# A gated cross-attention and mixture-of-experts block: preparation of the later batches spread anew over the engines, and batch 1 attended tile by tile

## The chip, the cores and the metric

One core of a Trainium2 chip runs the whole program. The metric is the device time of one execution in microseconds (us), lower is better. Engines are named as in the profile: PE is TensorE, DVE is VectorE, ACT is ScalarE, POOL is GpSimd, SP is SyncE, which here only starts transfers.

## The reference

x is 4 batches of 256 tokens with 256 features; ctx has the same shape.

```python
h  = layernorm(x)
xq = dequant(fp8(h))    # one scale for 128 features of a token
wq = dequant(fp8(ctx))  # one scale for a block of 128 x 128
x  = x + tanh(g_xattn) * einsum('emk,enk->emn', xq, wq)

h     = layernorm(x)
probs = softmax(h @ gate_w.T)       # 8 experts, top 4, renormalised
y_e   = (silu(h @ wg_e.T) * (h @ wu_e.T)) @ wd_e.T   # inner width 176
sh    = (silu(h @ swg.T) * (h @ swu.T)) @ swd.T      # inner width 704
out   = sum_e comb_e * y_e + sigmoid(h @ shared_gate_w.T) * sh
x     = x + tanh(g_ffn) * out
```

## The kernel before

The order on every engine is written out by hand, and semaphores join the engines. The work has two layers.

**Preparation**, once for each batch b of 0 to 3, two tiles of 128 tokens each. For x: moments (`stats_x`, DVE), inverse roots (`roots`, POOL), centring (`centre`, ACT), the largest magnitudes (`max_x`, DVE), scales (`scales_x`, DVE), scaling to the range of the 8-bit format (`scale_x`, ACT, four instructions). Then rounding to the grid of that format in float32: the exponent is masked out (`exponents_x`, DVE, L624), turned into a "magic number", 1.5 * 2^20 times the power of two, and this number is added and subtracted. For batches 1 to 3 of x and 0, 2, 3 of ctx the magic number is one more DVE instruction (`magic_x` L679, `magic_ctx` L642) and the addition and subtraction are two (`round_x` L685, L686, `round_ctx` L648, L649). For batch 0 of x and batch 1 of ctx ACT makes the magic number (`magic`, L377), and two DVE instructions of the scalar_tensor_tensor kind round with it (`rounded`, L628, L629). ctx has `max_ctx`, then a maximum over partitions by way of PE for two batches at once (`ctx_block_max`, `ctx_spread_max` on PE, `block_max_ctx`, `scales_ctx` on DVE), `scale_ctx` on ACT, and the same rounding.

The rounded x is transposed on PE (`transpose_xq`, L992), copied (`copy_xqt`, ACT, L381) and multiplied with ctx (`attend`, L1005) into two PSUM banks, one for each half k of the features. ACT scales the product of k = 0 into y2 (`residual0`, L388), DVE scales that of k = 1 and adds x (`residual1`, L710), DVE adds both (`residual_sum`, L717), and the second layernorm follows (`stats_x1`, `inverse_std1` on POOL L287, `norm_x1` L729), with transposes of x1 and of its normalised form y2 on PE. For batches 0 and 1 all this is a chain ahead of everything else, the prologue. In it `keep_clock_up(count)` (L1102) issues matrix products whose result nobody uses.

**Units.** The 2112 inner columns of all experts and of the shared layer are cut into 17 chunks, `UNITS`; they run twice, each time for half of the tokens (512, batches 0 and 1, then 2 and 3). Unit n has, on PE,

```python
            def unit(n):
                gate(n)
                up(n)
                down(n - 1)
```

each of six matrix products of 512 columns in float32 (three passes of high and low parts over two blocks, L1039, L1145 to L1153). Chunk 5 of each half, `SHORT`, has six and four in all. ACT makes the high parts of the weights (`high_gu` L434, `high_d` L438; `front` and `middle` issue them) and of the activations (`high_a`, L455), and the silu (L450); POOL makes the low parts of the weights (`low_gu` L293, `low_d` L299); DVE weighs the silu with the router's share (`mixed`, L788), multiplies by the up product (`gated`, L801; both are issued by `acts`) and makes the low part of the result (`low_a`, L810; for the short chunk the two are L797 and L807). What binds PE to them: `gate(n)` waits for `gu_lo_done` of its own weights and, as there is one bank GATE, for `mixed(n - 1)`; `down(n)` waits for `a_hi_done` and later `a_lo_done`.

The preparation of batches 2 and 3 is interleaved with units 2 to 15 in program order on each engine. The shared layer's result is weighed and added to x1t in `weigh_shared` (L829) and `add_shared` (L834), at units 6, 10 and 16 for the first half and at unit 23 for the second.

## Time and profile before

| | |
|---|---|
| median of 3 runs | 185.47 us (185.4 to 186.02) |
| the profiled execution | 185.45 us |
| its span in the profile | 183.0 us |
| PE busy | 158.4 us (87%) |
| DVE busy | 130.6 us (71%) |
| ACT busy | 101.9 us (56%) |
| POOL busy | 78.3 us (43%) |

The span is from the first to the last instruction that the profile shows; 2.45 us of the execution lie outside it. Times in the rows are from the start of the span. A matrix product's duration holds its way through the array, so that rows of PE overlap: what one costs is the distance between two starts. A row of the timeline is: start, duration, engine, line, operation, written tile and read tiles, count, and in brackets the idle time of the engine before it with what ended it.

### The profile page before, as it was taken

The page shows a single profiled execution, that of the slowest core. Times are in us where ns is not written, and L with a number is a line of the kernel's source. Part 1 is how long each engine was busy: PE and PEld are TensorE (multiplying, and loading weights), DVE is VectorE, ACT ScalarE, POOL GpSimd, SP SyncE. Part 2 cuts the span into 40 slices and gives each one's busy share as a digit, 9 for nine tenths or more (in the row PEclk, how much of TensorE's full clock was granted, in tenths as well). Part 3 has the DMA queues.
Part 4 walks back from the last instruction along what each step waited for, and adds up shares of the span by engine and source line. Part 5 has one row for each costly group of instructions (what it writes and reads, how often), then busy time and mean ns, then how long its engine had stood idle before and what let it go on. Part 6 is the DMA issues. An engine that isn't in the chain of part 4 may idle for free.

```text
span 183.0 us, 2355 instructions
## 1 busy us (share of the span) xinstructions
PE 158.4 (87%) x711; PEld 123.1 (67%) x711; DVE 130.6 (71%) x281; ACT 101.9 (56%) x220; POOL 78.3 (43%) x91
## 2 busy tenths in 40 slices
PE   0023999999996989998999999999998999999992
PEld 0011356877874867776788888888886888888871
DVE  1899994686878999999988755863478645554553
ACT  2568724488666865455765544595553555445430
POOL 4211244155764444440765443544554654544410
PEclk9999999999999999999999999999999999999999
DMA  4599900000299993222222222601999200000003
GB/s 130 147 407 400 378 4 0 5 0 4 97 264 231 343 402 131 86 59 86 86 90 86 86 88 86 206 0 53 217 266 324 89 5 0 0 0 0 0 0 115
DMA packets 11488, 22.74 MB, mean 124 GB/s; under 512 B 1986, under 2 KB 3010, under 8 KB 11476
## 3 DMA queue, kind: packets, MB, share of 16 engines
q1 hardware_dynamic: 10900, 22.07, 37.8%
q10 hardware_dynamic: 576, 0.52, 1.0%
q8 instruction: 5, 0.08, 0.2%
q14 instruction: 7, 0.06, 0.1%
HBM read 21.51 MB, written 1.09 MB: 123 GB/s over the span
## 4 chain that ended last, share of the span: by engine, by line
PE 53%; DVE 31%; issue 6%; ACT 5%; DMA 2%; POOL 1%; DVEq 1%; POOLq 0%
PE bank L1039 34%; DVE bank L801 4%; PE bank L1145 3%; DVE a_lo L810 3%; DVE silu L788 3%; PE bank L1149 2%; PE bank L1147 2%; PE bank L1146 2%; PE bank L1153 2%; PE bank L1152 2%; ACT a_hi L455 2%; DVE bn L596 2%; DMA x<-xs 2%; DVE x1t L834 2%; DVE x L710 1%
## 5 line engine op out<-in xcount | busy, mean ns | idle before, releaser
L293 POOL TENSOR_TENSOR w_lo<-w_raw,w_hi 128x512 fp32r<-128x512 f32 (+1 forms) x34 | 42.8, 1258 | 65.2 <-ACT w_hi L434 61.1
L1039 PE MATMUL bank<-h_hi,w_hi 128*128 128x512 f32 x130 | 52.2, 402 | 3.5 <-DVE silu L788 3.4
L1039 PE MATMUL bank<-h_hi,w_lo 128*128 128x512 f32 x130 | 50.8, 391 | 0.0
L1039 PE MATMUL bank<-h_lo,w_hi 128*128 128x512 f32 x130 | 50.7, 390 | 0.0
L455 ACT ACTIVATE a_hi<-bank 128x512 fp32r<-128x512 f32 (+1 forms) x34 | 20.3, 597 | 41.3 <-DVE bank L801 40.7
L299 POOL TENSOR_TENSOR w_lo<-w_raw,w_hi 128x256 fp32r<-128x256 f32 x34 | 26.1, 769 | 16.3 <-ACT w_hi L438 16.3
L1039 PEld LDWEIGHTS bank<-h_hi,w_hi 128*128 128x128 f32 x130 | 24.4, 188 | 10.7 <-issue 5.4
L801 DVE TENSOR_TENSOR bank<-silu,bank 128x512 f32<-128x512 f32 x32 | 22.2, 694 | 12.8 <-PE bank L1039 9.6
L810 DVE TENSOR_TENSOR a_lo<-bank,a_hi 128x512 fp32r<-128x512 f32 x32 | 22.0, 689 | 11.7 <-ACT a_hi L455 11.5
L1039 PEld LDWEIGHTS bank<-h_hi,w_lo 128*128 128x128 f32 x130 | 24.4, 188 | 5.3
L1039 PEld LDWEIGHTS bank<-h_lo,w_hi 128*128 128x128 f32 x130 | 24.5, 188 | 4.5
L788 DVE TENSOR_TENSOR silu<-bank,mix_b 128x512 f32<-128x512 f32 x22 | 15.1, 686 | 11.5 <-ACT bank L450 11.5
L434 ACT ACTIVATE w_hi<-w_raw 128x512 fp32r<-128x512 f32 (+1 forms) x34 | 20.8, 612 | 0.0
L450 ACT ACTIVATE bank<-bank 128x512 f32<-128x512 f32 x22 | 12.9, 585 | 10.0 <-PE bank L1039 10.0
L438 ACT ACTIVATE w_hi<-w_raw 128x256 fp32r<-128x256 f32 x34 | 13.9, 409 | 0.0
L1145 PE MATMUL bank<-a_hi,w_hi 128*128 128x512 f32 x32 | 12.6, 395 | 0.2 <-ACT a_hi L455 0.2
L1147 PE MATMUL bank<-a_hi,w_hi 128*128 128x512 f32 x32 | 12.5, 390 | 0.0
L1149 PE MATMUL bank<-a_lo,w_hi 128*128 128x512 f32 x32 | 12.5, 390 | 0.0
L1153 PE MATMUL bank<-a_lo,w_hi 128*128 128x512 f32 x32 | 12.5, 390 | 0.0
L1152 PE MATMUL bank<-a_hi,w_lo 128*128 128x512 f32 x32 | 12.5, 389 | 0.0
L1146 PE MATMUL bank<-a_hi,w_lo 128*128 128x512 f32 x32 | 12.5, 389 | 0.0
L976 PE MATMUL bank<-eye,amax_c 128*8 128x128 f32 x2 | 0.6, 324 | 9.4 <-DVE amax_c L590 9.4
(137 smaller groups left out, 215.3 us busy)
## 6 DMA issues: line engine op xcount, KB each, us to landing
w_raw<-w_full SPq DMA_DIRECT2D x32, 384.0 KB, 7.6
mix_b<-rows_dram SPq DMA_DIRECT2D x8, 256.0 KB, 6.5
out_t<-fin SPq DMA_DIRECT2D x4, 256.0 KB, 2.1
mix_b<-rows_dram SPq DMA_DIRECT2D x4, 224.0 KB, 6.1
mix_b<-rows_dram SPq DMA_DIRECT2D x4, 192.0 KB, 5.9
mix_b<-rows_dram SPq DMA_DIRECT2D x4, 160.0 KB, 5.9
x<-xs SPq DMA_DIRECT2D x2, 256.0 KB, 6.6
cw<-ctx_t SPq DMA_DIRECT2D x2, 256.0 KB, 7.0
```

Of the source, the lines that this page charges most:

```text
L293: nc.gpsimd.tensor_tensor(w_lo[:, n % 2, 0:cols], w_raw[:, n % RING, 0:cols], w_hi[:, n % 2, 0:cols].bitcast(F32), ALU.subtract).then_inc( ...
L299: nc.gpsimd.tensor_tensor(w_lo[:, n % 2, GU:WC], w_raw[:, n % RING, at:at + D], w_hi[:, n % 2, GU:WC].bitcast(F32), ALU.subtract).then_inc ...
L434: nc.scalar.activation(w_hi[:, n % 2, 0:cols], w_raw[:, n % RING, 0:cols], ACT.Copy).then_inc(gu_hi_done, 1)
L455: nc.scalar.activation(a_hi[0:rows, n % 2, :], UP[n % 2][0:rows, :], ACT.Copy).then_inc(a_hi_done, 1)
L788: nc.vector.tensor_tensor(silu[:, n % 2, :], GATE[:], mix_b[:, c, :], ALU.mult).then_inc(mixed_done, 1)
L801: nc.vector.tensor_tensor(UP[n % 2][:], silu[:, n % 2, :], UP[n % 2][:], ALU.mult).then_inc(act_done, 1)
L810: nc.vector.tensor_tensor(a_lo[:, n % 2, :], UP[n % 2][:], a_hi[:, n % 2, :].bitcast(F32), ALU.subtract).then_inc(a_lo_done, 1)
L1039: last = nc.tensor.matmul(out, w[k][a], x_of[k][b], start=(start and k == 0 and i == 0), stop=(stop and k == blocks - 1 and i == 2))
L1145: nc.tensor.matmul(OUT[0][:], w_hi[:, n % 2, cols[0]], a_hi[:, n % 2, :], start=start, stop=False)
L1146: nc.tensor.matmul(OUT[0][:], w_lo[:, n % 2, cols[0]], a_hi[:, n % 2, :], start=False, stop=False)
L1147: nc.tensor.matmul(OUT[1][:], w_hi[:, n % 2, cols[1]], a_hi[:, n % 2, :], start=start, stop=False)
L1149: done = nc.tensor.matmul(OUT[0][:], w_hi[:, n % 2, cols[0]], a_lo[:, n % 2, :], start=False, stop=stop)
```

## The change

- **Rounding.** `exponents_x` and, for batches 1 to 3, `exponents_ctx` now hand over to ACT, which makes the magic number (`magic_x`, `magic_ctx`), and `round_by_magic_x` and `round_by_magic_ctx` on DVE round with two scalar_tensor_tensor instructions. Five DVE instructions (x of batches 1, 2, 3, ctx of 2, 3) go and five on ACT come. ctx of batch 0 stays as it was.
- **Batch 1.** `attend_by_tiles(1)` multiplies token tile by token tile, into four bank halves in four banks (P1, P2, P0, OUT[1]), and reports each tile. Transposes of x1 of batches 0 and 1 go to UP[1] and UP[0]. `keep_clock_up` ahead of it has two products in place of four.
- **Sum of batch 0.** POOL does it (`residual_sum_0`) in place of DVE.
- **Weights.** `high_gu(0)`, `high_d(0)` and `high_gu(1)` stand later on ACT, behind `residual0(0)` and `residual0(1)`.
- **Batches 2 and 3.** The steps of preparation are placed anew in units 1 to 12 on DVE, ACT, POOL and PE. `add_shared` stands behind `low_a(16)` for the first half, and for the second its two instructions stand in units 24 and 25 in place of both ahead of unit 24.

```diff
-        ATT = ((UP[0], UP[1]), (P1, P2), (P0, P2), (P0, P2))
-        X1T = (OUT[1], P0, P1, P0)
+        ATT = ((UP[0], UP[1]), None, (P0, P2), (P0, P2))
+        ATT1 = ((P1, P2), (P0, OUT[1]))
+        X1T = (UP[1], UP[0], P1, P0)
         Y2T = (OUT[0], None, P1, P2)
         Y2T1 = (P1, OUT[1])
         LOGIT = (P0, P1)
...
         mixed_done, act_done = sem("mixed_done"), sem("act_done")
         a_hi_done, a_lo_done = sem("a_hi_done"), sem("a_lo_done")
         out_done, out_read, fin_done = sem("out_done"), sem("out_read"), sem("fin_done")
+
+        def attended(b):
+
+            return (1, 3, 4, 5)[b]
+
+        def att_view(b, k, jj):
...
+            def residual_sum_0():
+                pool.wait_ge(part0_done, 1)
+                pool.wait_ge(res0_ready, 1)
+                nc.gpsimd.tensor_tensor(x1[:, tile_slice(0), :], x1[:, tile_slice(0), :], y2[:, tile_slice(0), :], ALU.add)\
+                    .then_inc(x1_ready[0], 1)
+
             def low_gu(n):
...
             low_gate_w()
-            pool.wait_ge(cq_ready[1], 1)
+            residual_sum_0()
             low_gu(0)
             inverse_std1(0)
...
             low_d(3)
-            weights(4)
+            low_gu(5)
             roots(3)
+            low_d(4)
             for n in range(5, 13):
                 weights(n)
...
-            def magic(power, needs):
-
-                a.wait_ge(needs, 1)
+            def magic(power, powers, count):
+
+                a.wait_ge(powers, count)
                 a.wait_ge(least_filled, 1)
                 nc.scalar.activation(power, power, ACT.Relu, bias=least[:], scale=MAGIC).then_inc(magic_done, 1)
+
+            def magic_x(b, count):
+                magic(xe[:, tile_slice(b)].rearrange("p j k c -> p (j k c)"), power_x, count)
+
+            def magic_ctx(b, count):
+                magic(ce[:, b].rearrange("p k n c -> p (k n c)"), power_c, count)
 
             def copy_xqt(b):
                 a.wait_ge(xqt_psum, b + 1)
                 nc.scalar.activation(xqt[:, b], qt_view(b), ACT.Copy).then_inc(xqt_ready, 1)
 
             def residual0(b):
-                a.wait_ge(att_ready, b + 1)
                 a.wait_ge(deq_ready, b // HB + 1)
                 for jj, j in enumerate(tiles(b)):
+                    a.wait_ge(att_ready, attended(b) - (1 if b == 1 and jj == 0 else 0))
                     for n in range(2):
-                        last = nc.scalar.activation(y2[:, j, n * P:(n + 1) * P], ATT[b][0][:, jj * D + n * P:jj * D + (n + 1) * P],
-                                                    ACT.Copy, scale=deq[:, j, 0, n:n + 1])
+                        ns = slice(n * P, (n + 1) * P)
+                        last = nc.scalar.activation(y2[:, j, ns], att_view(b, 0, jj)[:, ns], ACT.Copy, scale=deq[:, j, 0, n:n + 1])
                 last.then_inc(res0_ready, 1)
 
             def copy_x1t(b):
...
-            magic(xe[:, tile_slice(0)].rearrange("p j k c -> p (j k c)"), power_x)
+            magic_x(0, 1)
             scale_ctx(0)
             scale_x(1)
             scale_ctx(1)
+            magic_x(1, 2)
             copy_xqt(0)
             high_gate_w()
+            magic_ctx(1, 1)
+            copy_xqt(1)
+            residual0(0)
             high_gu(0)
+            residual0(1)
             high_d(0)
             high_gu(1)
-            magic(ce[:, 1].rearrange("p k n c -> p (k n c)"), power_c)
-            copy_xqt(1)
-            residual0(0)
-            residual0(1)
             copy_x1t(0)
             copy_x1t(1)
...
             high_a(5)
+            scale_ctx(2)
             front(6)
             middle(6)
-            scale_x(3)
+            scale_x(2)
             high_a(6)
             front(7)
             middle(7)
-            scale_ctx(2)
+            magic_ctx(2, 2)
             high_a(7)
+            scale_x(3)
             front(8)
             middle(8)
+            magic_x(2, 3)
+            high_a(8)
             scale_ctx(3)
-            high_a(8)
             front(9)
             middle(9)
-            copy_xqt(2)
+            magic_x(3, 4)
             high_a(9)
             front(10)
             middle(10)
+            magic_ctx(3, 3)
+            copy_xqt(2)
             high_a(10)
             front(11)
-            copy_xqt(3)
             middle(11)
             high_a(11)
             residual0(2)
-            unit(12)
+            front(12)
+            middle(12)
+            copy_xqt(3)
+            high_a(12)
             front(13)
             middle(13)
...
-            def rounded(out, val, power, done):
-
+            def rounded(out, val, power, magics, done):
+
+                v.wait_ge(magic_done, magics)
                 after(did(nc.vector.scalar_tensor_tensor(val, power, LEAST, val, ALU.add, ALU.add)))
                 nc.vector.scalar_tensor_tensor(out, val, LEAST, power, ALU.subtract, ALU.subtract).then_inc(done, 1)
+
+            def round_by_magic_x(b, magics):
+                flat = "p j k c -> p (j k c)"
+                rounded(xq[:, tile_slice(b)].rearrange(flat), xc[:, tile_slice(b)].rearrange(flat),
+                        xe[:, tile_slice(b)].rearrange(flat), magics, xq_ready)
+
+            def round_by_magic_ctx(b, magics):
+                flat = "p k n c -> p (k n c)"
+                rounded(cq[:, b].rearrange("p k c -> p (k c)"), cw[:, b].rearrange(flat), ce[:, b].rearrange(flat),
+                        magics, cq_ready[b])
 
             def exponents_ctx(b):
                 v.wait_ge(ctx_scaled, b + 1)
                 last = exponents(ce[:, b].rearrange("p k n c -> p (k n c)"), cw[:, b].rearrange("p k n c -> p (k n c)"))
...
-
-            def round_x(b, magic_step):
-                flat = "p j k c -> p (j k c)"
-                val, mag = xc[:, tile_slice(b)].rearrange(flat), xe[:, tile_slice(b)].rearrange(flat)
...
-                after(did(nc.vector.tensor_tensor(val, val, mag, ALU.add)))
-                nc.vector.tensor_tensor(xq[:, tile_slice(b)].rearrange(flat), val, mag, ALU.subtract).then_inc(xq_ready, 1)
+                last.then_inc(power_x, 1)
 
...
+                    v.wait_ge(att_ready, attended(b) - (1 if b == 1 and jj == 0 else 0))
                     for n in range(2):
                         ns = slice(n * P, (n + 1) * P)
-                        last = nc.vector.scalar_tensor_tensor(x1[:, j, ns], ATT[b][1][:, jj * D + n * P:jj * D + (n + 1) * P],
+                        last = nc.vector.scalar_tensor_tensor(x1[:, j, ns], att_view(b, 1, jj)[:, ns],
                                                               deq[:, j, 1, n:n + 1], x[:, j, ns], ALU.mult, ALU.add)
+                if b == 0:
+                    last.then_inc(part0_done, 1)
+                    return None
                 return did(last)
 
...
-                    .then_inc(x1_ready, 1)
+                    .then_inc(x1_ready[b], 1)
 
             def stats_x1(b):
-                v.wait_ge(x1_ready, b + 1)
+                v.wait_ge(x1_ready[b], 1)
                 moments(1, x1, b)
                 nc.vector.tensor_scalar(ve1[:, tile_slice(b)], mv[:, 1, tile_slice(b), 1], LN_EPS, None, ALU.add)\
...
-            v.wait_ge(magic_done, 1)
-            flat_x, flat_c = "p j k c -> p (j k c)", "p k n c -> p (k n c)"
-            rounded(xq[:, tile_slice(0)].rearrange(flat_x), xc[:, tile_slice(0)].rearrange(flat_x),
-                    xe[:, tile_slice(0)].rearrange(flat_x), xq_ready)
+            round_by_magic_x(0, 1)
             mag_c0 = magic_ctx(0, exponents_ctx(0))
+            exponents_x(1)
             round_ctx(0, mag_c0)
-            mag_x1 = magic_x(1, exponents_x(1))
-            round_x(1, mag_x1)
             exponents_ctx(1)
             dequant_scales(0)
-            v.wait_ge(magic_done, 2)
-            rounded(cq[:, 1].rearrange("p k c -> p (k c)"), cw[:, 1].rearrange(flat_c), ce[:, 1].rearrange(flat_c), cq_ready[1])
-            residual_sum(0, residual1(0))
+            round_by_magic_x(1, 2)
+            round_by_magic_ctx(1, 3)
+            residual1(0)
             part_1 = residual1(1)
...
+            max_ctx(2)
+            max_ctx(3)
             acts(2)
             low_a(2)
             stats_x(2)
-            max_ctx(2)
             acts(3)
             low_a(3)
+            block_max_ctx(1)
             stats_x(3)
             acts(4)
+            scales_ctx(1)
             low_a(4)
-            max_ctx(3)
             scales_x(2, max_x(2))
             acts(5)
-            max_x_3 = max_x(3)
             low_a(5)
-            block_max_ctx(1)
-            scales_x(3, max_x_3)
+            scales_x(3, max_x(3))
             acts(6)
             weigh_shared(0)
             low_a(6)
-            scales_ctx(1)
+            exponents_ctx(2)
             acts(7)
-            exp_x2 = exponents_x(2)
-            mag_x2 = magic_x(2, exp_x2)
+            exponents_x(2)
+            dequant_scales(1)
             low_a(7)
-            exp_x3 = exponents_x(3)
-            mag_x3 = magic_x(3, exp_x3)
             acts(8)
-            round_x(2, mag_x2)
+            round_by_magic_ctx(2, 4)
             low_a(8)
-            exp_c2 = exponents_ctx(2)
-            mag_c2 = magic_ctx(2, exp_c2)
+            exponents_x(3)
             acts(9)
-            round_x(3, mag_x3)
+            round_by_magic_x(2, 5)
             low_a(9)
-            exp_c3 = exponents_ctx(3)
-            mag_c3 = magic_ctx(3, exp_c3)
+            exponents_ctx(3)
             acts(10)
-            round_ctx(2, mag_c2)
+            round_by_magic_x(3, 6)
             low_a(10)
-            dequant_scales(1)
-            shared_0 = [add_shared(0, 0)]
             acts(11)
-            round_ctx(3, mag_c3)
+            round_by_magic_ctx(3, 7)
             low_a(11)
             part_2 = residual1(2)
...
             gated(16)
-            shared_0.append(add_shared(0, 1))
             low_a(16)
+            shared_0 = [add_shared(0, 0), add_shared(0, 1)]
             acts(17)
             low_a(17)
...
             low_a(UNITS + SHORT + 1)
-            shared_1 = [add_shared(1, 0), add_shared(1, 1)]
-            for n in range(UNITS + SHORT + 2, 2 * UNITS):
+            acts(UNITS + SHORT + 2)
+            shared_1 = [add_shared(1, 0)]
+            low_a(UNITS + SHORT + 2)
+            acts(UNITS + SHORT + 3)
+            shared_1.append(add_shared(1, 1))
+            low_a(UNITS + SHORT + 3)
+            for n in range(UNITS + SHORT + 4, 2 * UNITS):
                 unit(n)
             finish(1, shared_1)
...
+            def attend_by_tiles(b):
+
+                pe.wait_ge(xqt_ready, b + 1)
+                pe.wait_ge(cq_ready[b], 1)
+                for jj in range(BT):
+                    for k in range(KC):
+                        last = nc.tensor.matmul(att_view(b, k, jj), xqt[:, b, k, jj * P:(jj + 1) * P],
+                                                cq[:, b, k, :], start=True, stop=True)
+                    last.then_inc(att_ready, 1)
 
             def transpose_tokens(b, src, dst, done):
...
                 pe.wait_ge(y2_ready, b + 1)
...
             transpose_xq(1)
-            keep_clock_up(4)
-            attend(1)
+            keep_clock_up(2)
+            attend_by_tiles(1)
             keep_clock_up(9)
             transpose_x1(0)
...
             transpose_comb(0)
+            ctx_block_max(1)
             unit(3)
-            unit(4)
-            unit(5)
-            ctx_block_max(1)
-            unit(6)
+            gate(4)
+            up(4)
             ctx_spread_max(1)
-            unit(7)
-            unit(8)
-            gate(9)
+            down(3)
+            for n in range(5, 10):
+                unit(n)
+            gate(10)
             transpose_xq(2)
-            up(9)
-            down(8)
-            unit(10)
-            transpose_xq(3)
+            up(10)
+            down(9)
             gate(11)
             up(11)
             attend(2)
             down(10)
-            unit(12)
+            gate(12)
+            transpose_xq(3)
+            up(12)
+            down(11)
             gate(13)
             transpose_x1(2)
```

## Rows read from the trace of the kernel before

**Rows 1.** The page: engines (part 1) and two groups of instructions (part 5).

```profile
PE 158.4 (87%) x711; PEld 123.1 (67%) x711; DVE 130.6 (71%) x281; ACT 101.9 (56%) x220; POOL 78.3 (43%) x91
...
L455 ACT ACTIVATE a_hi<-bank 128x512 fp32r<-128x512 f32 (+1 forms) x34 | 20.3, 597 | 41.3 <-DVE bank L801 40.7
```

**Rows 2.** Who PE waited for: us in total, times, longest.

```profile
PE bank L1039 <- DVE silu L788: 3.4, 5, 1.1
```

**Rows 3.** Chain that ended last, in order of time: start, us, what.

```profile
112.61 2.72 PE bank L1039 x12
```

**Rows 4.** Timeline of PE, the stretches in which it stood still.

```profile
56.92 0.47 PE L1140 MATMUL bank<-a_hi,w_hi 128*128 128x512 f32 x1 [0.52 <-DVE a_hi L807]
...
59.59 0.47 PE L1039 MATMUL bank<-h_hi,w_hi 128*128 128x512 f32 x1 [1.12 <-DVE silu L788]
...
70.51 0.40 PE L992 MATMUL bank<-eye_b,xq 128*128 128x128 bf16 x4 [0.36 <-DVE xq L686]
```

**Rows 5.** Timeline of DVE, units 8 and 9.

```profile
67.72 0.68 DVE L788 TENSOR_TENSOR silu<-bank,mix_b 128x512 f32<-128x512 f32 x1
...
69.04 0.68 DVE L685 TENSOR_TENSOR xc<-xc,xe 128x512 f32<-128x512 f32 x1
...
70.97 0.96 DVE L624 TENSOR_SCALAR ce<-cw 128x512 int32<-128x512 int32 x1
71.96 0.84 DVE L642 TENSOR_SCALAR ce<-ce 128x512 f32<-128x512 f32 x1
72.73 0.68 DVE L788 TENSOR_TENSOR silu<-bank,mix_b 128x512 f32<-128x512 f32 x1
```

**Rows 6.** Timeline of POOL, the same stretch.

```profile
70.36 1.29 POOL L293 TENSOR_TENSOR w_lo<-w_raw,w_hi 128x512 fp32r<-128x512 f32 x1 [2.84 <-ACT w_hi L434]
71.61 0.92 POOL L299 TENSOR_TENSOR w_lo<-w_raw,w_hi 128x256 fp32r<-128x256 f32 x1
```

**Rows 7.** Timeline of DVE and ACT, unit 5.

```profile
53.45 0.60 DVE L662 SCALAR_TENSOR_TENSOR safe_x<-amax_x,root 128x4 f32<-128x4 f32 x1
...
54.30 1.28 ACT L370 ACTIVATE xc<-xc,mul_x 128x128 f32<-128x128 f32 x4 [1.19 <-DVE mul_x L665]
```

**Rows 8.** Timeline of all engines, the prologue.

```profile
9.75 0.72 ACT L377 ACTIVATE xe<-xe,least 128x512 f32<-128x512 f32 x1
...
13.17 1.26 ACT L370 ACTIVATE xc<-xc,mul_x 128x128 f32<-128x128 f32 x4
13.76 0.43 DVE L642 TENSOR_SCALAR ce<-ce 128x512 f32<-128x512 f32 x1
...
19.01 0.69 DVE L628 SCALAR_TENSOR_TENSOR cw<-ce,cw 128x512 f32<-128x512 f32 x1 [0.24 <-ACT ce L377]
...
20.35 1.12 DVE L710 SCALAR_TENSOR_TENSOR x<-bank,deq,x 128x128 f32<-128x128 f32 x4
20.51 1.26 POOL L293 TENSOR_TENSOR w_lo<-w_raw,w_hi 128x512 fp32r<-128x512 f32 x1 [3.26 <-DVE cq L629]
21.50 0.82 DVE L717 TENSOR_TENSOR x<-x,y 128x512 f32<-128x512 f32 x1
...
23.28 0.73 DVE L596 BATCH_NORM_STATS2 bn<-x 128x6 f32<-128x256 f32 x2
...
27.28 0.73 DVE L729 TENSOR_SCALAR y<-x,mv,rstd 128x256 f32<-128x256 f32 x2 [0.27 <-POOL rstd L287]
```

**Rows 9.** Timeline of PE, the prologue.

```profile
18.35 1.91 PE L1102 MATMUL bank<-xqt,eye_b 128*128 128x512 bf16 x4
...
24.76 1.03 PE L1102 MATMUL bank<-xqt,eye_b 128*128 128x512 bf16 x4
...
29.08 0.47 PE L1075 MATMUL bank<-h_hi,gate_hl 128*128 128x512 f32 x1
```

**Rows 10.** Timeline of DVE and of PE, unit 23 and the start of gate(24).

```profile
137.35 2.50 DVE L834 SCALAR_TENSOR_TENSOR x1t<-fin,g_tanh,x1t 128x512 f32<-128x512 f32 x2
...
140.60 0.47 PE L1039 MATMUL bank<-h_hi,w_hi 128*128 128x512 f32 x1 [0.78 <-DVE silu L788]
```

More of the change, by code:

```diff
@@ L166, in flamingo_gated_block @@
         att_ready, res0_ready = sem("att_ready"), sem("res0_ready")
-        x1_ready, y2_ready = sem("x1_ready"), sem("y2_ready")
+        x1_ready, y2_ready = [sem(f"x1_ready{b}") for b in range(B)], sem("y2_ready")
+        part0_done = sem("part0_done")
         var1_ready, rstd1_ready = sem("var1_ready"), sem("rstd1_ready")
@@ L178, in flamingo_gated_block @@
         out_done, out_read, fin_done = sem("out_done"), sem("out_read"), sem("fin_done")
+        def attended(b):
+            return (1, 3, 4, 5)[b]
+        def att_view(b, k, jj):
+            return ATT1[jj][k][:, 0:D] if b == 1 else ATT[b][k][:, jj * D:(jj + 1) * D]
         def tiles(b):
@@ L512, in _ @@
             middle(5)
-            scale_x(2)
             high_a(5)
+            scale_ctx(2)
             front(6)
             middle(6)
-            scale_x(3)
+            scale_x(2)
             high_a(6)
@@ L633, in exponents_ctx @@
                 last = exponents(ce[:, b].rearrange("p k n c -> p (k n c)"), cw[:, b].rearrange("p k n c -> p (k n c)"))
-                if b == 1:
+                if b > 0:
                     last.then_inc(power_c, 1)
@@ L1001, in attend @@
                 if b == 3:
-                    pe.wait_ge(x1_ready, 3)
+                    pe.wait_ge(x1_ready[2], 1)
                 for k in range(KC):
                     for jj in range(BT):
-                        last = nc.tensor.matmul(ATT[b][k][:, jj * D:(jj + 1) * D], xqt[:, b, k, jj * P:(jj + 1) * P],
+                        last = nc.tensor.matmul(att_view(b, k, jj), xqt[:, b, k, jj * P:(jj + 1) * P],
                                                 cq[:, b, k, :], start=True, stop=True)
                 last.then_inc(att_ready, 1)
+            def attend_by_tiles(b):
[3 more added lines that the diff above has]
+                    for k in range(KC):
+                        last = nc.tensor.matmul(att_view(b, k, jj), xqt[:, b, k, jj * P:(jj + 1) * P],
+                                                cq[:, b, k, :], start=True, stop=True)
+                    last.then_inc(att_ready, 1)
             def transpose_tokens(b, src, dst, done):
@@ L1015, in transpose_x1 @@
             def transpose_x1(b):
-                pe.wait_ge(x1_ready, b + 1)
+                pe.wait_ge(x1_ready[b], 1)
                 if b == 2:
@@ L1028, in transpose_y2_by_blocks @@
                 pe.wait_ge(y2_ready, b + 1)
-                pe.wait_ge(x1t_copied, 1)
                 for k in range(KC):
```

10 lines of the change are left out of this document (removed).

## The prediction

> **What bounds the kernel now.** I read the page first, then who PE waited for, then PE's timeline for the places, then DVE, ACT and POOL around each place. PE is busy 158.4 of 183.0 us, the next engine DVE 130.6 [rows 1]. Twelve products in a row take 2.72 us, 0.227 us each [rows 3], so a full unit of 18 costs PE 4.08 us. PE is therefore the bound wherever its rows follow one another at this distance. It stands still in three stretches.
>
> First, the prologue: the first product that does lasting work in the units starts at 29.08 [rows 9]. The chain there is DVE's, from rounding through attention, the sum, the second layernorm.
>
> Second, units 5 to 12. PE waits 3.4 us in five places for `mixed` [rows 2], 0.78 of it in unit 24 [rows 10], which leaves 2.6 us in four places here, the longest 1.12. To these come 0.52 ahead of `down(5)` and 0.36 ahead of `transpose_xq(2)` [rows 4]. A product's row is 0.39 long where it costs 0.227, so each place loses 0.16 more than its idle time: 2.6 + 0.52 + 0.36 + 6 x 0.16 = 4.5 us. The reader is to see why in DVE's rows: from `mixed` of unit 8 to that of unit 9 are 72.73 - 67.72 = 5.01 us [rows 5], with no gap, against PE's 4.08. DVE is the bound of these units.
>
> Third, unit 24: 0.78 + 0.16 = 0.94 us lost, behind two `add_shared` that took 2.50 us [rows 10].
>
> **A price that matters throughout: DVE and POOL exclude each other.** The exponent step at 70.97 takes 0.96 us and ends at 71.93; POOL's `low_gu` has run since 70.36 and ends at 71.65 [rows 5, 6]. The same kind of instruction takes 0.43 with POOL idle [rows 8]. So it started only when POOL was through. In the other direction `low_d` takes 0.92 beside the DVE step at 71.96. A small step of `scales_x` is held 0.60 us in unit 5 [rows 7]. But `residual1`, whose product is read from PSUM, takes 1.12 with POOL's 20.51 to 21.77 on top of it [rows 8]. The Trainium skill, SBUF — State Buffer, section Who interferes with whom, has the rule: a DVE instruction in a two-port mode or with two SBUF inputs and a GpSimd instruction that reads SBUF lock each other out for a whole instruction; with at most one SBUF input and outside those modes it doesn't. By that rule the trace agrees. The rule speaks against expecting anything from scalar_tensor_tensor for its own sake: both roundings read two SBUF tensors and stay exposed.
>
> **Part A, the prologue.** After x of batch 0 is rounded, DVE masks ctx 0 and makes its magic number from 13.76 to 14.20 [rows 8], as before. The mask of x 1 now comes next and needs `scale_x(1)`, which ends at 13.17 + 1.26 = 14.43 [rows 8]: it starts at 14.46. It lies under the wait between steps, and `round_ctx(0)` follows with 0.35 + 0.72 + 0.60: the mask of ctx 1 starts at 16.13. Then 0.35, then `dequant_scales` to about 17.05. The magic numbers of x 1 and ctx 1 cost ACT 0.72 each [rows 8]; ACT makes the first from 15.5 and the second from 17.0, both before DVE asks. So DVE runs four rounding instructions without a gap, a pair in 20.35 - 19.01 = 1.34 us [rows 8]: 17.05 + 2.68 = 19.7. Before, `residual1(0)` started at 20.35; it gains 0.65: the removed magic instruction (0.46 with its hand-over), the 0.24 wait for ACT at 19.01, and small change. POOL's low part of the gate weights may hold one of them 0.2 to 0.3.
>
> `residual1(1)` can follow at 20.8: the products of batch 1 need xq 1 (18.45), its transposes, 0.6 of copying on ACT and then cq 1 at 19.8, and its first tile is there at about 20.4. What moved later on ACT is hidden: the copy of batch 0 comes 0.6 later and attention 0 with it, at 16.8, but its readers start at 19.6; `high_gu(0)` ends by 21.3, and the low part that PE wants at 28 lies on POOL in between.
>
> The sum of batch 0 takes DVE 0.82 [rows 8]; POOL has no such instruction in the trace. Nearest: POOL's subtraction of the same size, 1.26 with POOL alone. Below, 0.82 if POOL were as quick as DVE; above, 2.0 if a DVE instruction holds it first. I take 1.28, since kind and size are equal: 20.85 to 22.15. DVE's own sum stood at 21.50, but its statistics began only at 23.28, since `residual1(1)` was in between [rows 8]. They now begin at 22.15, 1.1 earlier. Then `low_gu(0)` runs on POOL to 23.4 and can hold the small step and `residual_sum(1)` for some 0.2. So the normalisation of batch 1, at 27.28 [rows 8], comes 0.9 to 1.1 earlier.
>
> PE must keep up. Four keep-up products before attention 1 took 1.91 us, 0.43 apart, and four later 1.03, 0.22 apart, both read as start to last end [rows 9]: the first run at the 1.2 GHz level, the later at 2.4, though the granted clock is shown full throughout. With two in place of four, attention 1 goes at 19.8 instead of 20.57. If the following nine stay slow to their end they take 3.9 and PE reaches the transposes of y2 about 0.3 late. I take 0.95 for part A; 0.3 (both POOL's sum and PE late) and 1.3 (no collision) are its bounds.
>
> **Part B, units 2 to 12.** Removed from DVE are four magic instructions here. In the unit of rows 5 it is 72.73 - 71.96 = 0.77 of the 5.01. The rest is 4.24 with the blocked mask, or 3.7 with an unblocked one, against PE's 4.08 and 0.2 to 0.4 of transposes or attention that the units carry. DVE stops being the bound, on the mean. The pass of maxima of ctx moves to unit 1 and 2, where DVE has waits; its small PE instructions cost as much in the new place. In unit 5, `gated(5)` no longer has `scale_x(2)` (1.28, [rows 7]) between it and `high_a(5)`, and DVE's second maximum is gone from ahead of `low_a(5)`: the 0.52 + 0.16 before `down(5)` goes.
>
> What is late next. (1) `mixed(6)` waits for its silu on ACT, which now stands behind `high_a(5)`, the 1.28 us of `scale_ctx(2)` and a weight instruction: following ACT from `gated(5)` on I get `gate(7)` about 0.4 late, against 1.12 + 0.16. (2) `transpose_xq(2)` stands behind `gate(10)`, which starts when `mixed(9)` ends and takes six products, 1.36 us. DVE in that time does `gated(9)` and the rounding pair, 0.65 + 1.34 = 2.0: PE waits 0.6, and more if POOL holds the pair. (3) Units 8 to 10: the weights of the next unit come behind a scaling or a magic number on ACT, and then need 1.29 on POOL; I allow 0.5 in all. So 1.5 of the 4.5 stays: gain 3.0. Bounds: 4.5 when nothing stays, 1.0 when each of the four magic numbers keeps ACT waiting for the mask and each rounding meets POOL once.
>
> ACT has 2.4 us of its own work for a unit at most (four instructions of at most 0.6, [rows 1]), plus 1.28 for a scaling, plus 0.72 for a magic number: 4.4 as an upper bound, with the narrow instructions less. That is close to a unit, and the reason why I keep 1.5.
>
> **Part C, unit 24.** One `add_shared` for a unit, each behind `gated` and ahead of a `low_a` whose result `down` wants more than a microsecond later. Two blocked ones took 2.50; one of 0.7 to 1.3 fits into the 1.2 that DVE waits in such a unit and that low part's slack. Gain 0.9, bounds 0 and 0.94. The first half's pair behind `low_a(16)` is hidden: DVE waits for PE there.
>
> **Sum.** 0.95 + 3.0 + 0.9 = 4.85 us. The profiled execution took 185.45, the median is 185.47; 185.45 - 4.85 = 180.6.
>
> **Rivals.**
> - *Locks and hand-overs eat half of part B.* For: DVE steps grew from 0.43 to 0.96 [rows 5] and the mask must now pass through ACT, where DVE once went on by itself. Against: DVE has other work between mask and rounding now. B falls to 1.0 to 1.7, A to 0.6: 181.9 to 184.
> - *Nothing is late.* If DVE runs ahead of `gate(10)` by 0.6 and ACT's order is as loose as its 56%: B is 4.2 to 4.5, total 178.7 to 179.6.
> - *Slower: ACT becomes the bound of units 6 to 11.* The place is a magic number ahead of `high_a(n)`: ACT waits for the mask, the mask waits for POOL, and `high_a`, the next weights and the next silu are queued behind it, on which POOL and DVE wait in turn. With A and C gained (1.85), the six units must lose 2.4 us more than now to end slower by 0.56, 0.4 in each on top of the 5.01 of unit 8, so that with the magic instruction gone from DVE each such wait must exceed about 1.2 us beyond its slack. The longest hold in these rows is 0.53 (0.96 against 0.43). Time then: 186 to 187.
> - *The change does not do what it says*: the prologue's gain is taken back by a slower sum on POOL, and in units 5 to 12 one wait replaces another. 185.
>
> **How the numbers follow.** Forecast 0.55 (its own range 179.6 to 181.9), nothing late 0.12, half of B 0.20, no change 0.05, slower 0.08. 178.8 to 183.6 leaves out the last two and an edge of two others. A measurement here can tell about 0.3%, 0.56 us: faster 0.87, same 0.05, slower 0.08.
>
> **What would show it.** Right: the first product of the units at about 28.1; `gate(13)` 3 to 4.5 us earlier than before; `mixed` to `mixed` below 4.5 us in units 8 to 10; no idle ahead of `gate(24)`; the rest shifted. Wrong: PE waits of 1 us and more for `a_hi` or `w_lo` in units 7 to 10, ACT idle ahead of L377, POOL's sum over 1.5 us, or keep-up products 0.43 apart up to the first real one.

## The result and the profile after

The changed kernel took 179.1 us (median of 4 runs, 178.6 to 179.66) against 185.44 us before: ratio 0.9656, 95% interval 0.9617 to 0.9695. It is 6.3 us faster (5.7 to 7.1). The forecast was 180.6, within 178.8 to 183.6, faster by 4.85. On another chip the same kernel later gave 0.9663 (0.9633 to 0.9693).

The page of the changed kernel, parts 1 and 5, and who PE waited for:

```profile
span 177.2 us, 2353 instructions
...
PE 155.8 (88%) x708; PEld 122.9 (69%) x709; DVE 123.4 (70%) x275; ACT 105.2 (59%) x225; POOL 79.0 (45%) x92
...
L477 ACT ACTIVATE a_hi<-bank 128x512 fp32r<-128x512 f32 (+1 forms) x34 | 20.3, 597 | 32.0 <-DVE bank L829 30.9
```

```profile
PE bank L1015 <- DVE xq L659: 3.4, 3, 2.4
...
PE bank L1071 <- POOL w_lo L308: 0.2, 1, 0.2
```

The wait of the products for `mixed`, 3.4 us in five places [rows 2], is gone; PE's 3.4 us for rounded x are 2.4 in the prologue, 0.7 there again and 0.3 in unit 10. DVE is 7.2 us less busy, ACT 3.3 more, POOL 0.7 more [rows 1].

The profiled execution took 178.96 us, 6.49 less than the 185.45 before; its span is 5.8 less, 177.2 against 183.0. The other 0.7 us lies outside the span, where the four executions of the changed kernel have anything from 1.8 to 2.5 us, so it is no gain that the trace can place. The span divides at three products. All times below are read the way the prediction did: a product costs the distance between two starts.

PE's timeline of the changed kernel: the first product of the units, `gate(3)`, the two small products of `ctx_spread_max(1)`, then the two places where it still stands still, then `gate(13)`:

```profile
28.41 0.47 PE L1107 MATMUL bank<-h_hi,gate_hl 128*128 128x512 f32 x1
...
41.70 0.47 PE L1071 MATMUL bank<-h_hi,w_hi 128*128 128x512 f32 x1
...
48.59 0.28 PE L1003 MATMUL bank<-eye,blk_w 128*128 128x8 f32 x2
48.73 0.48 PE L1177 MATMUL bank<-a_hi,w_hi 128*128 128x512 f32 x1
...
56.32 0.39 PE L1173 MATMUL bank<-a_hi,w_lo 128*128 128x512 f32 x1
...
56.91 0.50 PE L1071 MATMUL bank<-h_hi,w_hi 128*128 128x512 f32 x1 [0.20 <-POOL w_lo L308]
57.25 0.39 PE L1071 MATMUL bank<-h_lo,w_hi 128*128 128x512 f32 x1
...
70.85 0.39 PE L1071 MATMUL bank<-h_hi,w_lo 128*128 128x512 f32 x1
...
71.53 0.40 PE L1015 MATMUL bank<-eye_b,xq 128*128 128x128 bf16 x4 [0.29 <-DVE xq L659]
...
83.56 0.39 PE L1071 MATMUL bank<-h_hi,w_hi 128*128 128x512 f32 x1
```

And the same points of the kernel before, where rows 4 do not show them:

```profile
42.37 0.47 PE L1039 MATMUL bank<-h_hi,w_hi 128*128 128x512 f32 x1
...
57.69 0.40 PE L1141 MATMUL bank<-a_hi,w_lo 128*128 128x512 f32 x1
58.07 0.39 PE L980 MATMUL bank<-eye,blk_w 128*128 128x8 f32 x2
...
88.22 0.47 PE L1039 MATMUL bank<-h_hi,w_hi 128*128 128x512 f32 x1
```

- *Prologue.* The first product comes at 28.41 in place of 29.08 [rows 9]. But the first rounding started later, since the first x landed later: 12.31 in place of 11.93. From that rounding to the first product it is 16.10 us in place of 17.15: 1.05 gained.
- *Units 3 to 12.* From `gate(3)` (42.37) to `gate(13)` (88.22) it was 45.85 us; now it is 83.56 - 41.70 = 41.86: 4.0 gained. What is left of the stalls is 56.91 - 56.32 - 0.227 = 0.36 ahead of `gate(7)`, 71.53 - 70.85 - 0.227 = 0.45 ahead of `transpose_xq(2)`, and 0.05 and 0.04 ahead of `gate(9)` and `gate(10)`: 0.9 in all. Read in the same way, the kernel before loses 4.8, not the 4.5 of the prediction. The difference is at `gate(7)`: from 57.69 to 59.59 [rows 4] there lies one product (0.227) and the two small ones, which cost 48.73 - 48.59 = 0.14 where nothing stalls, so 1.53 us are lost there, where 1.12 + 0.16 were counted.
- *Unit 24.* The 0.94 us stall [rows 10] is gone.

Together 6.0 of the trace, or 5.6 of the 5.8 by which the span is shorter, since the first rounding came 0.38 later.

DVE's timeline of the changed kernel, `mixed` of units 7 to 9 and the steps of unit 8 between them:

```profile
60.15 0.68 DVE L816 TENSOR_TENSOR silu<-bank,mix_b 128x512 f32<-128x512 f32 x1
...
64.39 0.69 DVE L816 TENSOR_TENSOR silu<-bank,mix_b 128x512 f32<-128x512 f32 x1 [1.36 <-ACT bank L472]
...
65.72 0.77 DVE L658 SCALAR_TENSOR_TENSOR cw<-ce,cw 128x512 f32<-128x512 f32 x1
...
67.74 0.42 DVE L653 TENSOR_SCALAR xe<-xc 128x512 int32<-128x512 int32 x1
...
68.65 0.69 DVE L816 TENSOR_TENSOR silu<-bank,mix_b 128x512 f32<-128x512 f32 x1 [0.48 <-ACT bank L472]
```

From `mixed` to `mixed` it is now 4.2 to 4.3 us, where it was 5.01 [rows 5], and DVE waits for ACT's silu 1.36 and 0.48 us: it is no longer the bound.

### The profile page after: what moved, and what is told of

Same layout as the page of the kernel before. It is cut to its first block, busy times and chain, and to the rows that moved or that the text cites. A ratio compares the mean times of both kernels' runs of the same rounds, so it can differ in the third digit from the quotient of the medians.

```text
span 177.2 us, 2353 instructions
## 1 busy us (share of the span) xinstructions
PE 155.8 (88%) x708; PEld 122.9 (69%) x709; DVE 123.4 (70%) x275; ACT 105.2 (59%) x225; POOL 79.0 (45%) x92
## 4 chain that ended last, share of the span: by engine, by line
PE 60%; DVE 20%; ACT 9%; issue 5%; DMA 2%; POOL 2%; DVEq 1%; POOLq 0%
PE bank L1071 36%; DVE bank L829 3%; PE bank L1177 3%; PE bank L1181 3%; PE bank L1179 3%; PE bank L1178 3%; PE bank L1184 3%; PE bank L1185 3%; DMA x<-xs 2%; DVE bn L625 2%; ACT cw L378 2%; DVE a_lo L838 2%; DVE silu L816 2%; ACT a_hi L477 1%; ACT xc L386 1%
## 5 line engine op out<-in xcount | busy, mean ns | idle before, releaser
L314 POOL TENSOR_TENSOR w_lo<-w_raw,w_hi 128x256 fp32r<-128x256 f32 x34 | 25.5, 750 | 17.0 <-ACT w_hi L460 17.0
L625 DVE BATCH_NORM_STATS2 bn<-x 128x6 f32<-128x256 f32 x16 | 5.9, 412 | 4.8 <-DMA x<-xs 4.4
```

Of the source, the lines that this page charges most:

```text
L314: nc.gpsimd.tensor_tensor(w_lo[:, n % 2, GU:WC], w_raw[:, n % RING, at:at + D], w_hi[:, n % 2, GU:WC].bitcast(F32), ALU.subtract).then_inc ...
```

## The experiments

All ratios are to the kernel before, measured on the same chip; the changed kernel stood at 0.9656 and 0.9663, 0.001 is about 0.19 us.

### The three parts, each alone

**Prologue alone.** The changed kernel with units 1 to 16 and the shared layer as before.

```diff
 # units: the lists of all engines as before, magic_x and magic_ctx of batches 2 and 3 on VectorE
-            exponents_x(2)
+            exp_x2 = exponents_x(2)
+            mag_x2 = magic_x(2, exp_x2)
...
-            round_by_magic_x(2, 5)
+            round_x(2, mag_x2)
```

> Only the prologue of the changed kernel (rounding of x 1 by ScalarE's magic number, batch 1 by tiles, the sum of batch 0 on GpSimd, later weights); units and shared layer as before. Additive theory: the new kernel's first product came 1.05 us earlier counted from the first rounding, so 1.0 to 1.1 us faster than before, 184.4. Rival, that the units' start is set by something else and gives it back: 185.2 or more.

Measured: 184.25 us against 185.29, ratio 0.9954 (0.9930 to 0.9978), median difference 1.0 us.

**Unit 24 alone.** The kernel before with

```diff
-            shared_1 = [add_shared(1, 0), add_shared(1, 1)]
-            for n in range(UNITS + SHORT + 2, 2 * UNITS):
+            acts(UNITS + SHORT + 2)
+            shared_1 = [add_shared(1, 0)]
+            low_a(UNITS + SHORT + 2)
+            acts(UNITS + SHORT + 3)
+            shared_1.append(add_shared(1, 1))
+            low_a(UNITS + SHORT + 3)
+            for n in range(UNITS + SHORT + 4, 2 * UNITS):
                 unit(n)
```

> Only the two add_shared of the second half in units 24 and 25. Additive theory: the 0.94 us stall ahead of gate(24) goes and nothing else moves, 184.5. Rival, that each add_shared is blocked by POOL and stalls its own unit: 185.0 to 185.5.

Measured: 184.29 us, 0.9947 (0.9922 to 0.9971), 1.0 us faster. DVE's timeline of this kernel:

```profile
139.70 0.75 DVE L834 SCALAR_TENSOR_TENSOR x1t<-fin,g_tanh,x1t 128x512 f32<-128x512 f32 x1
...
143.78 0.75 DVE L834 SCALAR_TENSOR_TENSOR x1t<-fin,g_tanh,x1t 128x512 f32<-128x512 f32 x1
```

Two instructions take 1.5 us in place of 2.50 [rows 10]. Behind `gated` they do not meet POOL; together, ahead of the unit, both did (POOL's low parts ran from 136.87 to 139.30, the pair from 137.35 to 139.85). PE has no idle time ahead of `gate(24)` in this kernel, nor in the changed one.

**Units alone.** The kernel before with the units' lists of all engines and the four magic numbers on ACT as in the changed one, prologue and unit 24 as before.

```diff
 # units 1 to 16: the lists of all engines as in the changed kernel
-            mag_x2 = magic_x(2, exp_x2)
...
+            round_by_magic_ctx(2, 3)
```

> Only units 2 to 16 as in the changed kernel (the four magic numbers on ScalarE and all placements there); prologue and unit 24 as before. Additive theory: what A (1.05) and C (0.94) leave of the 6.3 us, so 4.2 to 4.4 us faster, 181.1. Rival, that part B was worth the predicted 3.0 and A or C more: 182.4.

Measured: 180.75 us, 0.9757 (0.9725 to 0.9790), 4.5 us faster. So the parts are worth 1.0, 1.0 and 4.5, 6.5 in sum against 6.3 for the whole: they add up, within what can be measured (each of the first two is known to some 0.4 us, the third to 0.6). The additive theory stands, and part B is where the forecast was too low. In the trace of this kernel `gate(3)` to `gate(13)` takes 84.33 - 42.49 = 41.84 us, as in the changed kernel, 4.0 less than before.

### Inside the units: less work on DVE, or another place for it?

**Placement without the magic numbers.** The changed kernel with

```diff
-            exponents_ctx(2)
+            mag_c2 = magic_ctx(2, exponents_ctx(2))
...
-            round_by_magic_ctx(2, 4)
+            round_ctx(2, mag_c2)
 # and likewise x of batches 2 and 3 and ctx of batch 3; ScalarE's four magic numbers go
```

> The changed kernel with the four magic numbers of batches 2 and 3 back on VectorE right behind their masks (and rounding in two tensor_tensor), at the new places. If taking work off VectorE is what freed the units: each of units 6 to 10 has 0.5 to 0.9 us more on VectorE, over TensorE's 4.08, and 1.5 to 2.5 us come back: 180.6 to 181.6. Rival, that the new placement alone does it: within 0.5 us of the changed kernel, 179.1 to 179.6.

Measured: 179.93 us, 0.9713 (0.9681 to 0.9746), some 1.0 us slower than the changed kernel (0.9713 against 0.966, the mean of its two ratios). The intervals overlap, but the spans of all four executions are 178.0 to 178.2, those of the changed kernel 176.7 to 177.2, and in the trace `gate(3)` to `gate(13)` takes 84.64 - 41.58 = 43.06 us, 1.2 more than there. That lies between the two theories, nearer to placement: by the ratios some 3.5 of the 4.5 us, in the traces 2.8 of the 4.0, come without taking a single magic number off DVE.

**Magic numbers without the placement.** The kernel before with

```diff
             high_a(7)
+            magic_x(2, 2)
             front(8)
             middle(8)
+            magic_x(3, 3)
             scale_ctx(3)
...
-            mag_x2 = magic_x(2, exp_x2)
...
-            round_x(2, mag_x2)
+            round_by_magic_x(2, 3)
 # and likewise for x 3, ctx 2 and ctx 3, each at its old place
```

> The kernel before with the four magic numbers of batches 2 and 3 made by ScalarE and two-instruction rounding, every step else at its old place. Placement theory (undoing only the magic numbers cost 0.8 of the 6.3 us): the two stalls around units 5 and 6 stay, 2.0 us, and the later ones shrink by some 0.8 to 1.5: 183.8 to 184.5. Rival, my recorded step, that taking 0.77 us of each unit off VectorE frees units 8 to 12 by itself: all 2.5 us of their stalls go, 182.8.

Measured: 183.49 us against 185.77, 0.9875 (0.9855 to 0.9896), 2.3 us faster. That is the recorded step's 2.5 rather than placement's 0.8 to 1.5. The two edits overlap: 2.3 + 3.5 is more than 4.5. The traces show in what. A stop is here the distance between two starts less what the products between them cost:

| kernel | `gate(3)` to `gate(13)`, us | stops at `down(5)` and `gate(7)` | later stops, up to `gate(13)` |
|---|---|---|---|
| before | 88.22 - 42.37 = 45.85 | 2.2 | 2.6 |
| magic numbers alone | 85.85 - 42.43 = 43.42 | 2.2 | 0.4 |
| placement alone | 84.64 - 41.58 = 43.06 | 0.4 | 1.7 |
| changed | 83.56 - 41.70 = 41.86 | 0.4 | 0.5 |

PE's timeline with the magic numbers alone moved:

```profile
56.98 0.47 PE L1153 MATMUL bank<-a_hi,w_hi 128*128 128x512 f32 x1 [0.50 <-DVE a_hi L828]
...
59.65 0.47 PE L1052 MATMUL bank<-h_hi,w_hi 128*128 128x512 f32 x1 [1.13 <-DVE silu L809]
```

These two stand as before [rows 4], and behind them the largest up to `gate(13)` is 0.22 us, at 81.56. With placement alone the early ones go and later ones stay. DVE, POOL and PE in unit 7:

```profile
59.01 1.10 DVE L649 TENSOR_SCALAR ce<-cw 128x512 int32<-128x512 int32 x1
59.78 0.92 POOL L314 TENSOR_TENSOR w_lo<-w_raw,w_hi 128x256 fp32r<-128x256 f32 x1
60.14 0.84 DVE L678 TENSOR_SCALAR ce<-ce 128x512 f32<-128x512 f32 x1
...
61.73 0.47 PE L1082 MATMUL bank<-h_hi,w_hi 128*128 128x512 f32 x1 [0.56 <-DVE silu L827]
```

A mask and a magic number one behind the other, both held by POOL (1.10 and 0.84 where each takes 0.43 alone), still make a stall of 61.73 - 60.78 - 0.227 = 0.72 us; with the mask alone in that place (59.13, 1.10 us) the changed kernel has none. So: the stops of units 8 to 12 go almost wholly by the magic numbers alone and by a third through the placement alone; of those ahead of `down(5)` and `gate(7)`, 2.2 us, 1.8 go by the placement, and none by the magic numbers. Which of the moves in the placement does it, the maxima, the masks or the order on ACT and PE, was not tested one by one.

**Is it ACT's order in unit 5?** The changed kernel with

```diff
-            high_a(5)
             scale_ctx(2)
+            high_a(5)
```

> The changed kernel with scale_ctx(2) ahead of high_a(5), as scale_x(2) stood before. If that order made the 0.52 us idle ahead of down(5): high_a(5) comes 1.28 us later, has 0.6 of slack, so 0.5 to 0.7 us slower in the stall, the rest of the units absorbing little: 179.7. Rival, that VectorE alone was the cause: 179.1.

Measured: 179.0 us, 0.9644 (0.9622 to 0.9667), no slower than the changed kernel. ACT, DVE and PE of this kernel:

```profile
52.03 0.70 DVE L825 TENSOR_TENSOR bank<-silu,bank 64x512 f32<-64x512 f32 x1
52.17 1.27 ACT L378 ACTIVATE cw<-cw,scl_c 128x128 f32<-128x128 f32 x4
...
53.34 0.58 ACT L477 ACTIVATE a_hi<-bank 64x512 fp32r<-64x512 f32 x1
...
53.96 0.68 DVE L835 TENSOR_TENSOR a_hi<-bank,a_hi 64x512 fp32r<-64x512 f32 x1 [1.22 <-ACT a_hi L477]
...
55.25 0.39 PE L1172 MATMUL bank<-a_hi,w_hi 128*128 128x512 f32 x1
```

`scale_ctx(2)` runs from 52.17, most of it beside `gated(5)`, and `down(5)` at 55.25 has no idle time ahead of it: the low part was ready at 54.6. Without DVE's lateness there is no stall: before, `gated(5)` started at 54.29, 25.2 us after the first product, behind `max_ctx(3)`, `max_x(2)` and a `scales_x` step held by POOL [rows 7]; here it starts 52.03 - 27.98 = 24.05 us after it. The rival is right that this is enough for `down(5)`, but it does not follow that ACT's order had no part. `high_a(5)` starts 53.34 - 52.73 = 0.6 us after `gated(5)` ends here, and in the kernel before it was 0.5 late behind `scale_x(2)`:

```profile
55.48 0.57 ACT L455 ACTIVATE a_hi<-bank 64x512 fp32r<-64x512 f32 x1
```

`gated(5)` had ended there at 54.99. DVE is 25.2 - 24.05 = 1.15 us earlier now, more than the whole stall of 0.67. Mending ACT's order alone, which by these rows would take up to 0.5 of it, was not tried. The order is not quite free now either: `gate(7)` comes 56.79 - 27.98 = 28.81 us after the first product in place of 56.91 - 28.41 = 28.50, 0.3 us that the times do not show. (The first x landed at 3.96 in this profiled execution and at 4.39 in the changed kernel's, and every later time moves with it.)

### Inside the prologue

Three edits of the changed kernel, each undoing one thing. The sum of batch 0 back on DVE:

```diff
-            residual_sum_0()
...
-            residual1(0)
+            residual_sum(0, residual1(0))
             part_1 = residual1(1)
```

> The changed kernel with the sum of batch 0 back on VectorE ahead of residual1(1). If POOL's sum matters: statistics of batch 0 no sooner but VectorE has 0.7 us more ahead of batch 1's: 0.5 to 0.7 us slower than the changed kernel, 179.7. Rival, that the early attention and rounding gave the 1.0 us and the sum nothing: 179.1.

Batch 1 reported together:

```diff
-                for jj in range(BT):
-                    for k in range(KC):
+                for k in range(KC):
+                    for jj in range(BT):
...
-                    last.then_inc(att_ready, 1)
+                last.then_inc(att_ready, 2)
```

> The changed kernel with the four products of batch 1 reported together, in the order of before (same four banks). If the report by tile is what lets residual1(1) follow residual1(0) without a gap: the second tile is done 0.5 us after the first, and residual1(0) ends 0.8 us after the products start, so at most 0.3 us slower. Rival, that the early start of the products alone does it: no difference, within 0.2 us of the changed kernel.

Four keep-up products ahead of it:

```diff
-            keep_clock_up(2)
+            keep_clock_up(4)
             attend_by_tiles(1)
```

> The changed kernel with four keep-up products ahead of batch 1 in place of two. They run 0.43 us apart, so attention of batch 1 starts at 20.3 to 20.6 + 0.38 in place of 20.28 and residual1(1) after it waits some 0.3 us: 0.2 to 0.6 us slower than the changed kernel. Rival, that they cost nothing since the statistics wait for POOL's sum anyway, and TensorE comes sooner to its 2.4 GHz level: no difference.

Together with the last two ran the changed kernel once more; the sum on DVE ran on another chip.

> The changed kernel unaltered, as the measure for the other three on the same chip: 0.9656 of the time before, 179.1 to 179.4.

| kernel | ratio to before (95% interval) | first rounding to first product, us |
|---|---|---|
| changed | 0.9663 (0.9633 to 0.9693) | 28.44 - 12.36 = 16.08 |
| sum on DVE | 0.9653 (0.9629 to 0.9678) | 28.31 - 11.93 = 16.38 |
| batch 1 together | 0.9666 (0.9636 to 0.9696) | 28.45 - 12.17 = 16.28 |
| four keep-up products | 0.9657 (0.9630 to 0.9685) | 28.29 - 12.04 = 16.25 |
| before | 1 | 29.08 - 11.93 = 17.15 |

No time differs from the changed kernel's. In the traces the prologues are 0.2 to 0.3 us longer, too little for the measured times. With batch 1 together the statistics of batch 0 start as early as in the changed kernel, and the 0.2 arises on PE behind them (last section), so the report by tile is worth nothing that shows. Of the four keep-up products 0.2 to 0.6 us were expected, and 0.17 shows in the trace. The miss is the sum: 0.5 to 0.7 us were expected of it. The changed kernel shows why it is worth so little:

```profile
20.05 2.15 DVE L735 SCALAR_TENSOR_TENSOR x<-bank,deq,x 128x128 f32<-128x128 f32 x8
...
21.29 1.27 POOL L302 TENSOR_TENSOR x<-x,y 128x512 f32<-128x512 f32 x1 [3.12 <-DVE x L735]
...
22.59 0.75 DVE L625 BATCH_NORM_STATS2 bn<-x 128x6 f32<-128x256 f32 x2 [0.39 <-POOL x L302]
```

DVE saves its own 0.6 to 0.8 us but then waits 0.39 for POOL's 1.27. So most of the 1.05 us is the rounding chain (`residual1(0)` 0.68 us earlier from the first rounding: 20.05 - 12.31 = 7.74 against 20.35 - 11.93 = 8.42); the rest comes in pieces of 0.2 to 0.3 that the traces show and no timing here separates.

### A version faster than both

The two stalls left are taken on by their positions.

```diff
 # TensorE
             gate(10)
-            transpose_xq(2)
             up(10)
+            transpose_xq(2)
             down(9)
 # ScalarE
             high_a(5)
-            scale_ctx(2)
             front(6)
             middle(6)
-            scale_x(2)
+            scale_ctx(2)
             high_a(6)
             front(7)
             middle(7)
+            scale_x(2)
             magic_ctx(2, 2)
```

> The changed kernel with its two left stalls taken on: scale_ctx(2) behind middle(6) and scale_x(2) behind middle(7) on ScalarE, transpose_xq(2) behind up(10) on TensorE. If the waits of gate(7) for low_gu(7) (0.37 us) and of transpose_xq(2) for rounding (0.46) come from these positions, 0.8 us faster than the changed kernel: 178.3. Rival, that a new wait takes their place (gate(8) for its weights, attend(2) for the copy): 179.0.

Measured: 178.01 us against 185.77, 0.9587 (0.9563 to 0.9611). By the ratios that is 1.3 to 1.4 us faster than the changed kernel (0.9656 and 0.9663), by the spans of the traces, 176.1 against 177.2, 1.1. Not all of this is the moves': 0.4 of the 1.1 is the first x, which landed at 3.99 in place of 4.39 and with which neither has to do. From `gate(3)` to `gate(13)` it is 82.49 - 41.30 = 41.19 us in place of 41.86, so 0.7 us is what the trace shows of them, where 0.8 was expected; the rest of the 1.3 stays open. PE at `gate(3)`, the two places and `gate(13)`:

```profile
41.30 0.47 PE L1071 MATMUL bank<-h_hi,w_hi 128*128 128x512 f32 x1
...
55.96 0.39 PE L1173 MATMUL bank<-a_hi,w_lo 128*128 128x512 f32 x1
...
56.24 0.47 PE L1071 MATMUL bank<-h_hi,w_hi 128*128 128x512 f32 x1
```

```profile
71.61 0.39 PE L1071 MATMUL bank<-h_hi,w_lo 128*128 128x512 f32 x1
...
71.84 0.40 PE L1015 MATMUL bank<-eye_b,xq 128*128 128x128 bf16 x4
...
82.49 0.39 PE L1071 MATMUL bank<-h_hi,w_hi 128*128 128x512 f32 x1
```

0.28 and 0.23 apart, where a product costs 0.227: both stalls are gone. One small one is new, 64.70 - 64.34 - 0.227 = 0.13 ahead of `gate(9)`. With only the move of `transpose_xq(2)`:

> The changed kernel with only transpose_xq(2) behind up(10). If its position made the 0.46 us stall and the restart of TensorE after it: 0.5 us faster than the changed kernel, and the other 0.5 to 0.8 of the version with both moves belongs to ScalarE's order. Rival, that attend(2) or the copy inherits the wait: no difference.

Measured: 178.48 us, 0.9638 (0.9606 to 0.9670). The median is 0.5 us below that of the changed kernel measured beside it (178.48 against 179.0), as expected, but the intervals overlap; the trace bears it out: a span of 176.7 against 177.2, and 83.10 - 41.75 = 41.35 us from `gate(3)` to `gate(13)`, 0.5 less.

## Why the prediction was right, and where it was off

The forecast's direction and range held, its mechanism in the main, and its own sum was 1.5 us short. The measured 179.1 lies outside the 179.6 to 181.9 that the forecast gave itself and inside the 178.7 to 179.6 of the rival "nothing is late", of whose two conditions the first did not come about: `transpose_xq(2)` still waited 0.45. Of the 1.5 us the traces place 1.1, nearly all in part B.

- **Part A, 0.95 us taken: 1.05 in the trace, 1.0 alone.** The rounding chain gained 0.68 where 0.65 was worked out. The price of POOL's sum, 1.28 taken from a subtraction of the same size, was 1.27, and the statistics behind it came 1.07 earlier from the first rounding (10.28 in place of 11.35), where 1.1 was worked out. But the sum's own share is 0.3 in the trace. That the nine keep-up products might stay slow to their end and make PE late was rightly seen: in the kernel with batch 1 together they took 3.86 us and the first product came 0.2 later, in the changed kernel 2.71.
- **Part C, 0.9 us taken: the 0.94 gone, 1.0 alone.**
- **Part B, 3.0 us taken: 4.0 in the trace, 4.5 alone.** This is the mis-sized term, at both of its ends. Of the 1.5 us that were said to stay, 0.9 did: item 1 (`gate(7)`, 0.4) measured 0.36 and item 2 (`transpose_xq(2)`, 0.6) 0.45. Item 3, 0.5 us for weights that come late in units 8 to 10, measured 0.1, since POOL's low part came just in time for `gate(9)`:

```profile
63.95 1.30 POOL L308 TENSOR_TENSOR w_lo<-w_raw,w_hi 128x512 fp32r<-128x512 f32 x1 [3.12 <-ACT w_hi L456]
...
65.31 0.50 PE L1071 MATMUL bank<-h_hi,w_hi 128*128 128x512 f32 x1
```

  And the 4.5 us that it was to be taken from were 4.8, as said above of `gate(7)`. So 4.8 - 0.9 = 3.9 of the trace's 4.0. ACT, which was to be near its bound in these units and the reason to keep 1.5, still waited 0.5 us and more for DVE in each of them (0.76 at 60.27, 0.61 at 61.59, 0.54 at 65.85, 0.54 at 70.10). The other 0.5 us, between 4.0 in the trace and 4.5 in the median, is inside the interval of that ratio (3.9 to 5.1) and stays open.
- **The reason given for part B was half of it.** The prediction said that DVE stops being the bound because four magic numbers leave it. Alone that is worth 2.3 us (2.4 in the trace); undone, it costs 1.0 (1.2). The placement alone is worth 3.5 by the ratios and 2.8 in the trace. The likely reason, argued from the rows and not tested move by move, is that it has the maxima done where DVE waits and spreads the masks.
- **The claim on unit 5** held in its result and in its part on DVE, which alone is enough. What the order on ACT did alone is open: with a scaling put back there no stall came, since DVE was 1.2 us earlier.
- **The rivals.** That locks eat half of part B did not happen, though the locks did: the mask of ctx 2 took 1.10 us, that of ctx 3 0.91. Behind the first of them DVE waited for ACT soon after, 1.36 us at 64.39, so it had slack to give. The longest hold in the rows shown, 0.53, was not the longest of the kernel before: its mask at 65.42 took 1.50, 1.07 more than alone. ACT's wait for the masks, named as a sign of being wrong, did come, twice 0.76 us, and did no harm that shows; 1.2 was the price from which it would have counted.
- **The signs.** The first product came at 28.41 for 28.1, with x 0.38 late. `gate(13)` came 4.66 earlier, a little over the 3 to 4.5 that were named. `mixed` to `mixed` was 4.2 to 4.3, and ahead of `gate(24)` there was no idle time.

## What to carry to other kernels

When one engine's queue feeds the bound engine, list its work unit by unit and compare each unit with the bound engine's 4.1 us, not the total with the total: here the same instructions in other places, among them the maxima in units 1 and 2 and the masks from unit 6 on, gave 2.8 of the 4.0 us in the traces. Taking work off that queue and spreading it can be worth the same microseconds, so test each alone before paying for both. Then read the stalls that are left and move the one instruction that stands ahead of each; two moves gave another 0.7 us in the trace. Before a span is compared with a span, look when the first input landed: that alone moved these by 0.4 us.

## What the runs showed of the hardware

- After a stop of PE, however short, and after its transposes, the first two products start 0.30 to 0.34 us apart in place of 0.227 (56.91 to 57.25 above), 0.07 to 0.11 more. From `gate(3)` to `gate(13)` that is ten places before and eight now, 0.80 and 0.77 us in all: fewer long stops did not make it cheaper, since short ones and transposes took their place.
- The keep-up products change from 0.43 to 0.22 us apart, that is from the 1.2 to the 2.4 GHz level, at different times in near-equal kernels, after much the same work of PE. In the changed kernel the wider spacing ends by 22.3; with batch 1 reported together it lasts to 24.0, although PE's work from 18.86 and 18.71 on is the same in both but for the order of the four products of batch 1:

```profile
22.34 0.96 PEld L1134 LDWEIGHTS bank<-xqt,eye_b 128*128 128x128 bf16 x5 [0.25 <-issue]
```

```profile
23.93 0.15 PEld L1134 LDWEIGHTS bank<-xqt,eye_b 128*128 128x128 bf16 x1 [0.28 <-issue]
```

  The granted clock of the profile is full in both. The statistics of batch 0 came at the same distance from the first rounding (10.28 and 10.27 us) in both, and the 0.2 us by which the second kernel's first product is later lies behind them, in PE, which came 0.5 late to the first transposes of y2 (26.80 - 12.17 = 14.63 from the first rounding, against 26.40 - 12.31 = 14.09). So the level cost this prologue 0.2 us.
- The moment at which the first x landed differs by 0.5 us between profiled executions (3.96 to 4.43), whatever the kernel.
